# A block of attention mix and quantised linear layer on one core: the mix's units worked in two phases, and the work on ACT and VectorE spread anew

## The reference

```python
attn = jnp.einsum('ds,td->st', w1, w2) * sparse_mask        # 1024 x 1024, a band
y = jnp.einsum('bds,st->bdt', x, attn) + b2
x = layernorm(x + gelu(y))
# w_l: 4-bit weights, decoded from bit planes through a table of 16 values a row
# w_h: the same with 8 bits, used for tokens whose norm exceeds 64
y = where(norm(x) > 64, x @ w_h.T, x @ w_l.T) + bias
x = layernorm(x + y)
```

## Time and profile before

| | |
|---|---|
| time, median of 3 runs | 298.35 us (298.05 to 298.6) |
| the profiled execution | 298.25 us |
| its span | 296.4 us |
| PE busy | 281.9 us (95%) |
| DVE busy | 217.9 us (73%) |
| ACT busy | 195.7 us (66%) |
| POOL busy | 88.5 us (30%) |
| the mix | 35.4 to 89.8 us of the span |
| start of the linear layer (L571) | 93.6 us |

### The profile page before, as it was taken

The page is one execution under the profiler, slowest core; times in us unless marked ns, Lnnn a source line. Parts: engine busy times, 40 slices in busy tenths (PEclk is TensorE's granted clock), DMA queues, the critical chain, the costliest instruction groups (busy, mean ns, idle before and its releaser), DMA issues.

```text
span 296.4 us, 4898 instructions
## 1 busy us (share of the span) xinstructions
PE 281.9 (95%) x1835; PEld 245.8 (83%) x1835; DVE 217.9 (73%) x355; ACT 195.7 (66%) x257; POOL 88.5 (30%) x152
## 2 busy tenths in 40 slices
PE   8899989899999999999999999999999999999980
PEld 4688866667668999999999999999988778888880
DVE  1679999897868977997979686295578586763371
ACT  2866368988999979989989985362447446222110
POOL 4000001533353202121520000000387866766421
PEclk9999999999999999999999999999999999999995
DMA  6999999999999611111111111174188663434323
GB/s 211 400 358 358 377 376 333 246 247 243 205 196 195 138 35 53 38 35 55 35 56 35 45 45 38 54 160 197 64 260 287 226 212 141 140 115 155 123 114 111
DMA packets 28479, 49.76 MB, mean 168 GB/s; under 512 B 2464, under 2 KB 11936, under 8 KB 28448
## 3 DMA queue, kind: packets, MB, share of 16 engines
q1 hardware_dynamic: 23392, 40.53, 40.1%
q0 software_dynamic: 4352, 8.39, 15.8%
q10 hardware_dynamic: 704, 0.46, 0.5%
HBM read 36.79 MB, written 12.58 MB: 167 GB/s over the span
## 4 chain that ended last, share of the span: by engine, by line
PE 60%; ACT 8%; DVE 8%; SPq 7%; DMA 6%; POOL 5%; issue 5%; DVEq 0%; ACTq 0%
PE acc L571 14%; PE acc L573 14%; PE acc L572 14%; PE acc L500 4%; DMA w<-in_w2d 3%; PE acc L475 2%; SPq L286 2%; ACT leaf L745 2%; ACT zz L788 2%; PE acc L510 2%; PE acc L476 2%; PE acc L477 2%; DMA off_band<-in_mask_rest 2%; SPq L285 1%; DVE leaf L1032 1%
## 5 line engine op out<-in xcount | busy, mean ns | idle before, releaser
L571 PE MATMUL acc<-lin,zz 128*128 128x256 f32 (+2 forms) x424 | 130.6, 308 | 0.3 <-issue 0.3
L573 PE MATMUL acc<-lin,zz 128*128 128x256 f32 (+2 forms) x424 | 129.8, 306 | 0.0
L572 PE MATMUL acc<-lin,zz 128*128 128x256 f32 (+2 forms) x424 | 129.5, 306 | 0.0
L571 PEld LDWEIGHTS acc<-lin,zz 128*128 128x128 f32 x424 | 80.1, 189 | 4.5 <-issue 0.5
L572 PEld LDWEIGHTS acc<-lin,zz 128*128 128x128 f32 x424 | 80.2, 189 | 3.9
L573 PEld LDWEIGHTS acc<-lin,zz 128*128 128x128 f32 x424 | 80.0, 189 | 4.1
L745 ACT ACTIVATE leaf<-planes,lut,flip 128x1024 f32<-128x1024 uint8 x56 | 67.5, 1236 | 1.2 <-DVE dest L1032 1.2
L1032 DVE COPY_PREDICATED leaf<-planes,leaf 128x1024 f32<-128x1024 uint8 x32 | 43.5, 1360 | 14.0 <-ACT leaf L745 13.3
L1493 POOL DMA_DIRECT2D z<-in_xr x16 | 19.5, 1224 | 70.8 <-ACT z L727 68.2
L854 ACT ACTIVATE junk<-rows,cols 128x1024 bf16<-128x1024 f32 x15 | 17.2, 1146 | 35.1 <-POOL cols L1467 35.1
L1032 DVE COPY_PREDICATED dest<-planes,leaf 128x1024 f32<-128x1024 uint8 x24 | 32.5, 1356 | 3.7 <-ACT leaf L745 2.3
(11 more groups left out here) (118 smaller groups left out, 438.4 us busy)
## 6 DMA issues: line engine op xcount, KB each, us to landing
z<-in_xt SPq DMA_DIRECT2D x16, 512.0 KB, 8.7
z<-in_xr POOLq DMA_DIRECT2D x16, 512.0 KB, 8.5
out_rows<-rows SPq DMA_DIRECT2D x15, 512.0 KB, 2.9
out_rows<-parts SPq DMA_DIRECT2D x32, 128.0 KB, 1.7
rows<-out_rows SPq DMA_DIRECT2D x16, 256.0 KB, 2.7
w<-in_w1d SPq DMA_DIRECT2D x7, 512.0 KB, 9.0
off_band<-in_mask_rest SPq DMA_DIRECT2D x8, 448.0 KB, 4.7
w<-in_w2d SPq DMA_DIRECT2D x3, 584.0 KB, 9.5
```

The source lines that it names most:

```text
L571: nc.tensor.matmul(bank, hi, w_hi, start=k == 0, stop=False)
L572: nc.tensor.matmul(bank, hi, w_lo, start=False, stop=False)
L573: last = nc.tensor.matmul(bank, lo, w_hi, start=False, stop=k == KB - 1)
```

## The change

The order of PE in a group becomes: units 0 to 3, three pieces on 64 rows; units 4 to 7, and all other pieces on 64 rows. `beside(g, 1)` opens the second lot, but in group 0 it lies in the first, so that the gelus of units 0 and 1 can be done before `turn(0)`. `BESIDE`, from which all waits are worked out, follows. On ACT and DVE `x_hi(0, 2)` goes from DVE to ACT, the decode steps get other numbers (14 in all as before) and places, the roundings of z stand right after the first steps of their group, and `xe_lo` stands behind `x_lo` of r = 0 and 1.

```diff
-    X_ON_ACT = (1, 3)
+    X_ON_ACT = [(1, 2, 3), (1, 3), (1, 3), (1, 3)]
-    MIX_STEPS = [(3, 3), (2, 1), (2, 1), (2, 0)]
+    MIX_STEPS = [(2, 2), (4, 0), (2, 0), (3, 1)]
-    BESIDE = (0, 2, 1, 3, 5, 4, 6)
+    BESIDE = (2, 0, 1, 5, 3, 4, 6)
...
# PE
+                beside(g, 2)
                 excess(g, 0)
                 beside(g, 0)
-                beside(g, 2)
-                for t in (4, 5, 6):
+                if g == FIRST_TURN_GROUP:
+                    beside(g, 1)
+                for t in (4, 5, 6, 7):
                     own(g, t)
-                excess(g, 1)
-                beside(g, 1)
-                beside(g, 3)
-                beside(g, 5)
-                own(g, 7)
                 if g == FIRST_TURN_GROUP:
                     pe.wait_ge(consts_made, 4)
                     turn(0)
+                excess(g, 1)
+                if g != FIRST_TURN_GROUP:
+                    beside(g, 1)
+                beside(g, 5)
+                beside(g, 3)
                 excess(g, 2)
                 beside(g, 4)
                 beside(g, 6)
...
# ACT
+            make_x_hi(0, 2)
             make_x_hi(0, 3)
             for g in range(GROUPS):
                 gelu(g, 0)
-                done = decode_steps(MIX_STEPS[g][0], done)
-                if g + 1 < GROUPS:
+                if g == FIRST_TURN_GROUP:
+                    done = decode_steps(1, done)
+                    gelu(g, 1)
+                    gelu(g, 2)
+                    done = decode_steps(MIX_STEPS[g][0] - 1, done)
+                    make_lin_hi(0)
+                    done = decode_steps(MIX_STEPS[g][1], done)
                     make_xe_hi(g + 1)
-                gelu(g, 1)
+                else:
+                    done = decode_steps(MIX_STEPS[g][0], done)
+                    for pair in MIX_Z.get(g, ()):
+                        make_z_hi(*pair)
+                    if g + 1 < GROUPS:
+                        make_xe_hi(g + 1)
+                    gelu(g, 1)
+                    gelu(g, 2)
                 if g + 1 < GROUPS:
                     make_x_hi(g + 1, 1)
-                if g == FIRST_TURN_GROUP:
-                    make_lin_hi(0)
-                gelu(g, 2)
-                gelu(g, 3)
-                for pair in MIX_Z.get(g, ()):
-                    make_z_hi(*pair)
-                done = decode_steps(MIX_STEPS[g][1], done)
-                gelu(g, 4)
-                gelu(g, 5)
+                for t in (3, 4, 5):
+                    gelu(g, t)
                 if g + 1 < GROUPS:
                     make_x_hi(g + 1, 3)
                 gelu(g, 6)
                 if g + 1 == GROUPS:
                     make_lin_hi(1)
                 gelu(g, 7)
+                if g != FIRST_TURN_GROUP:
+                    done = decode_steps(MIX_STEPS[g][1], done)
...
# DVE
                 done = decode_steps(MIX_STEPS[g][0], done)
-                if g + 1 < GROUPS:
-                    make_xe_lo(g + 1)
-                    make_x_lo(g + 1, 0)
-                    make_x_lo(g + 1, 1)
                 for pair in MIX_Z.get(g, ()):
                     make_z_lo(*pair)
-                if g == FIRST_TURN_GROUP:
-                    make_lin_lo(0)
-                if g != GROUPS - 2:
-                    done = decode_steps(MIX_STEPS[g][1], done)
                 if g + 1 < GROUPS:
+                    make_x_lo(g + 1, 0)
+                    if g == FIRST_TURN_GROUP:
+                        make_lin_lo(0)
+                    make_x_lo(g + 1, 1)
+                    if g == FIRST_TURN_GROUP:
+                        done = decode_steps(MIX_STEPS[g][1], done)
+                    make_xe_lo(g + 1)
                     make_x_lo(g + 1, 2)
                     make_x_lo(g + 1, 3)
                 else:
                     make_lin_lo(1)
-                if g == GROUPS - 2:
+                if g != FIRST_TURN_GROUP:
                     done = decode_steps(MIX_STEPS[g][1], done)
```

More of the change, by code:

```diff
@@ L996, in make_x_lo @@
             def make_x_lo(g, r):
-                if r in X_ON_ACT:
-                    dve.wait_ge(x_hi_made, len(X_ON_ACT) * g + X_ON_ACT.index(r) + 1)
+                if r in X_ON_ACT[g]:
+                    dve.wait_ge(x_hi_made, sum(len(pairs) for pairs in X_ON_ACT[:g]) + X_ON_ACT[g].index(r) + 1)
                 else:
@@ L1003, in make_x_lo @@
                     nc.vector.tensor_copy(x_hi[:, 2 * r:2 * r + 2, :], z[:, g, 2 * r:2 * r + 2, :]).then_inc(x_rounded, 1)
-                    dve.wait_ge(x_rounded, (PAIRS - len(X_ON_ACT)) * g + r // 2 + 1)
+                    here = [pair for pair in range(PAIRS) if pair not in X_ON_ACT[g]]
+                    dve.wait_ge(x_rounded, sum(PAIRS - len(pairs) for pairs in X_ON_ACT[:g]) + here.index(r) + 1)
                 nc.vector.tensor_tensor(x_lo[:, 2 * r:2 * r + 2, :], z[:, g, 2 * r:2 * r + 2, :],
```

## The result

The changed kernel takes 301.83 us (median of 5 runs, 300.3 to 301.91) against 298.6 us for the kernel before on the same chip (298.05 to 298.96): ratio 1.0089, interval 1.0072 to 1.0107. It is slower, as forecast, but by 3.2 us between the medians (2.7 us by the ratio) instead of 1.05, and it lies above the range. The profiled execution took 301.83 us, its span is 300.0 us, 3.6 more than before.

What follows compares the result with a forecast made beforehand. PE sets the pace, ACT has little to spare; later queues delay group 2 by 0.1 us, group 3 by 0.95, the linear stage by 1.4. Taken as +1.2 on 298.25: 299.4 us, range 297.2 to 300.9.

Steps and rivals of the forecast that it cites:

- the chain through the queues: Mix: ACT's and DVE's new orders delay group 2 by 0.1 us, group 3 by 0.95, the linear stage by 1.4.
- the merges are the heart of it: DVE, group 1: four merges ahead of `x_lo(2,0)` instead of two make group 2 start at 65.38 against 65.26 us.
- `xe` comes late: Rival, chance 0.10: later `xe_lo(1)` delays group 2's `xe_raw` load; at 9.9 us, `own(2,2)` about 2 late, 301.4 us.
- the sum: Whole kernel: the three terms less a little, +1.2 us on the profiled 298.25, forecast 299.4 us.
- The wait of `beside(4)`: PE, each group: `beside(4)` follows `beside(3)` with only `excess(2)` between, at most 0.1 us a group.
- The stall of `beside(1)` in group 0: PE, group 0: `beside(1)` directly follows `beside(0)`, 0.54 us instead of 0.23, a stall of 0.31.
- the earlier place of the `z` roundings gives nothing: Group 3 and way out: Gram sums no longer wait for group 0's `z` roundings, but the linear part waits for `lin_lo`.
- The first rival: Mix: PE stays the bound if DVE and ACT keep up; at most 296.4 us, more likely 297.4; chance 0.22.
- The cap of 1.9 us: After the mix: `turn(3)` waits for decoding, which only ACT's 1.9 us of idle can move forward, limiting the gain.

Runs made afterwards that it cites:

- Feed: xe_own with `x_hi(1,1)` earlier on ACT and one decode step of group 1 put at its end; 297.22 us, ratio 0.995 to the kernel before.
- feed_z_shared: feed_z with `xe_raw` of group 3 in the shared buffer, as in the changed kernel; 303.5 us, ratio 1.0149 to the kernel before.
- feed_z: Feed with the `z_hi` pair of group 2 ahead of its decode steps on ACT; 296.56 us, ratio 0.9927 to the kernel before.
- full2: feed_z with ACT's group 3 reordered: centring, `z_hi` pair, gelus 1 to 3, leaf, gelus 4 and 5, `lin_hi(1)`, rest; 296.2 us, ratio 0.9917.
- xe_own: Changed kernel with an own buffer for group 3's `xe_raw`, loaded ahead of its x; 300.01 us, ratio 1.0054 to the kernel before.
- pe_only: Kernel before with PE's new order alone, ACT's and DVE's tables and queues as they were; 304.0 us, ratio 1.0178.

## Why the prediction was wrong

**Right: the chain through the queues.** `turn(0)` came 10.60 us after the mix's start (forecast 45.79 − 35.37 = 10.42), group 2 after 30.29 (30.01), group 3 13.10 after group 2 (13.1), DVE stood idle 2.50 us before `x_lo(1,1)` (2.5), `turn(1)` waited 0.42 (0.6). With the load's wait taken out, the mix is 59.93 us, where the forecast had 95.0 − 35.37 = 59.6. Feed shows that this chain sets the start of group 2: with one of the four merges ahead of `x_lo(2,0)` taken away and `x_hi(1,1)` earlier, it is −2.9 us. By an estimate from rows, 1.65 us of it is DVE's shorter idle (2.50 to 0.85) and 1.36 the merge; the two edits were not tried apart, so that the merges are the heart of it, as the prediction held, is not shown.

**Failed: "`xe` comes late" was weighed for one load and not for the next.** The step that failed is in this rival, and the sum had no term for it. The rival priced the load of `xe_raw` for group 2, which was issued at 55.91 and came in time, and it set the slow load aside because "the slow one had loads of x ahead of it in its queue, this one has none". But the slow one, the load for group 3, is still there, and it still has the loads of x ahead of it. Both things that it hangs on moved behind DVE's merges: its own release `xe_lo(2)`, from 61.41 to 67.47, and through `xe_lo(1)` the loads of x, whose first went out at 56.30 instead of 49.99. It landed at 78.35 instead of 72.07, while ACT's own use moved by 4 us only (78.36 less the wait of 2.13 is 76.23, before 72.23). ACT stood 2.13 us, PE then 1.20 at `own(3,2)`. The rows for it were there: the slowest landing of 9.9 us and ACT's use at 72.23, so at most 0.2 us of slack. Worth: about 1.3 us of the median; ACT waited 2.1 and 0.9 us in two executions of the changed kernel.

Of the two, the traces speak for the loads of x. In all seven profiled executions in which the load for group 3 stands behind them, it landed 1.8 to 2.2 us after the last of them, while it took anything from 7.7 to 13.0 us from its own issue. And in feed_z_shared, with its issue 4.2 us earlier, it gained only what the last load of x gained (1.1 us) and 0.2 more. So the prediction's 9.9 us was no property of the load.

The Trainium skill (DMA: Bandwidth & Descriptors, Anatomy of one DMA — SWDGE (gpsimd) path) fits one DMA issued by GpSimd with 2.0 us and the bytes at 436 GB/s, which would be 2.6 us for these 256 KB by an estimate. The loads here are issued by SP and took 5.1 to 10.1 us in the changed kernel, so the fit does not describe them, and the measurement decides.

**A size off: the start of the mix.** 0.9 us of the profiled difference, and none of the change's. It shows in the kernel before as well.

**A size off: two small terms.** The wait of `beside(4)` cost 0.19 us a group, not at most 0.1. So a group bound by PE got 0.2 us shorter (12.26 to 12.1) and not 0.4. The stall of `beside(1)` in group 0 was well put: 42.57 to 43.14 is 0.57 us, where 0.54 was forecast. Here the hand-over counted: with the lone matmul of the Trainium skill alone (TensorE: Matmul & The Clock Gate, Single matmul latency), 379 ns for 512 columns, the stall would have been 0.15 by an estimate, and 0.57 less 0.23 is 0.34.

**Wrong, without effect on the sum: "the earlier place of the `z` roundings gives nothing".** Back in their old place they cost the Gram sums 1.2 us. The sum of the changed kernel did not need it, the reading of what to undo did.

**The first rival** held that PE's saving shows if the queues follow. They did not in the changed kernel; in feed_z they do, and PE's order gives 1.58 us there. That this is near the 1.6 of its eight changes is luck: net of the new stall, a group gains 0.2 us, and most of the 1.58 is waits that the old order has with these queues. The cap of 1.9 us that I drew from ACT's idle time did not show: the mix of feed_z is 2.1 us shorter than before and `turn(3)` waits 0.2 us as ever. Some of it shows in full2, whose `turn(3)` waits 0.6.

**Open.** The order of landings in SP's queue speaks for a backlog that the load must sit out. But no run moved the loads of x alone, or the issue of the load alone (xe_own does both), so this is read from the traces and not shown by an experiment. Why the last load of x takes 11.3 us before and 17.4 us now, issued at nearly the same time, stays open too; the three ahead of it were issued later than before, and POOL's DMAs ran beside them.

## What to carry to other kernels

When a step moves, follow everything that it releases to its next user, one round further than the group in which the step stands: a single-buffered load whose release sits behind other work in an in-order queue is a deadline too. Its slack is the time from its landing to its use. Where it will land after a change can't be had from its issue and its time from issue to landing alone: look also at what stands ahead of it in its queue and when that lands. An order that is better for the bounding engine pays only together with feeder queues that can follow: here the same edit of PE's order made the mix 5.5 us longer with the old queues and 1.6 us shorter with queues that follow. The first figure holds 1.5 us of a fallen clock: a wait of PE can cost more than its own length. Before the loss is put down to the idea, try the idea with its feeders mended.

## What the hardware showed that was not expected

A load of 256 KB took between 3.1 and 13.0 us from issue to landing in one execution (feed_z_shared, same shape, same queue), and an issue 4.2 us earlier than in the changed kernel brought the landing forward by 1.3 only. In seven executions of five kernels the load for group 3 landed 1.8 to 2.2 us behind the load of x ahead of it; the DMA share of groups 2 and 3 stands at 1.08 to 1.12 in either kernel.

TensorE's granted clock stayed at 1.00 throughout the mix in twelve of the fourteen profiled executions. It fell to 0.50 (1.2 GHz of 2.4) in pe_only, for about 3.5 us behind a wait of 1.97 us and the turn, and in feed_z_shared, for about 6.7 us behind a wait of 2.68 us, three matmuls and most of a wait of 1.91 us. It did not fall behind the wait of 1.85 us at 56.32 in pe_only. At the lower level 512 columns take 0.43 us from start to start instead of 0.23.

The wait on the load varied by 1.2 us between two executions of the changed kernel. The start of the mix varied by 0.8 between two executions of either kernel and by 1.2 over all, while the distances between the starts of the groups repeated within 0.1 us.
